# Order of the last mixture's gathers, its mix and three weight loads in the start of the last attention of a four-layer kernel

## What is computed

```python
x = x + tanh(g_xattn[i]) * xattn_i(layernorm(x), ctx)     # i = 0..3
x = x + tanh(g_ffn[i])   * ffn_i(layernorm(x))
```

## Time and profile before

| | before |
|---|---|
| median of 3 runs | 776.3 us (774.14 to 778.49) |
| the profiled execution, whole | 768.22 us |
| its span, first to last instruction | 766.1 us |
| mean granted TensorE clock | 0.925 of full |
| busy: PE / PE weight loads / DVE / ACT / POOL | 660.2 / 552.0 / 450.2 / 399.3 / 311.9 us |
| chain that ended last, by engine | PE 65%, DVE 18%, POOL 6%, issue 4%, ACT 3%, DMA 3% |
| the stretch in question | about 630 to 675 us of the 766 |

### The profile page before, as it was taken

How to read it: one execution, slowest core, us unless ns; L and a number is a source line. 1 busy time by engine, 2 the same in 40 slices (tenths; PEclk the granted TensorE clock), 3 DMA queues, 4 the chain that set the end, 5 groups by cost and what they waited for, 6 DMA issues and landing times.

```text
span 766.1 us, 17361 instructions
## 1 busy us (share of the span) xinstructions
PE 660.2 (86%) x6445; PEld 552.0 (72%) x6445; DVE 450.2 (59%) x1400; ACT 399.3 (52%) x977; POOL 311.9 (41%) x266
## 2 busy tenths in 40 slices
PE   3698997879989899899999999784699868999894
PEld 2487775779989777688887854563489857777684
DVE  5375768732223668575656677655433335779693
ACT  4565542355546565465656567321155745666471
POOL 4654430826234276132232347402234447654041
PEclk9699998699999999999999999985599988999997
DMA  6643680856776210000000020003357653521001
GB/s 169 162 99 90 195 241 2 245 154 173 219 223 188 85 31 25 1 2 1 1 1 2 1 83 1 1 0 96 116 138 228 174 161 98 144 56 37 3 15 42
DMA packets 60716, 70.92 MB, mean 93 GB/s; under 512 B 7051, under 2 KB 40859, under 8 KB 60635
## 3 DMA queue, kind: packets, MB, share of 16 engines
q1 hardware_dynamic: 57563, 63.52, 29.4%
q0 software_dynamic: 3072, 6.30, 2.7%
HBM read 48.89 MB, written 20.91 MB: 91 GB/s over the span
## 4 chain that ended last, share of the span: by engine, by line
PE 65%; DVE 18%; POOL 6%; issue 4%; ACT 3%; DMA 3%; SPq 0%; POOLq 0%; ACTq 0%; DVEq 0%
PE banks L1475 9%; PE banks L1491 8%; PE banks L1609 4%; PE banks L1312 3%; PE banks L1201 3%; PE banks L1618 3%; PE banks L1629 3%; PE banks L1289 3%; PE banks L1159 3%; PE banks L1161 2%; PE banks L1160 2%; PE banks L1267 2%; PE banks L1301 2%; PE banks L1661 2%; DVE rr L1955 2%
## 5 line engine op out<-in xcount | busy, mean ns | idle before, releaser
L994 ACT ACTIVATE hT<-banks,wup 128x128 f32<-128x128 f32 x304 | 86.8, 369 | 72.1 <-PE banks L1475 71.9
L913 ACT ACTIVATE pT<-banks 77x512 f32<-77x512 f32 x128 | 69.1, 591 | 54.8 <-PE banks L1289 54.4
L719 POOL DMA_INDIRECT xs<-xn,slot x48 | 47.0, 979 | 100.0 <-DVE ysb L2273 50.1
L624 POOL TENSOR_TENSOR kbd<-k,const 96x1248 fp32r<-96x1248 f32 x32 | 72.8, 2285 | 32.7 <-PE banks L1289 30.2
L1475 PE MATMUL banks<-xTs,wup 128*128 128x128 f32 x608 | 83.7, 283 | 2.1 <-issue 2.1
L1491 PE MATMUL banks<-wd,hT 128*128 x608 | 81.8, 279 | 0.6 <-ACT hT L994 0.3
L1475 PEld LDWEIGHTS banks<-xTs,wup 128*128 128x128 f32 x608 | 77.3, 200 | 3.0 <-issue 2.7
L679 POOL TENSOR_TENSOR sh<-sh,rd 128x616 f32<-128x616 f32 x32 | 39.0, 1218 | 98.8 <-DVE rd L1912 98.7
L2273 DVE COPY ysb<-banks 128x128 f32<-128x128 f32 x76 | 22.1, 291 | 91.7 <-PE banks L1491 91.7
L1491 PEld LDWEIGHTS banks<-wd,hT 128*128 128x128 f32 x608 | 74.7, 194 | 1.3 <-issue 1.1
L604 POOL TENSOR_TENSOR rstd<-vv,const 128x4 f32<-128x4 f32 x24 | 25.5, 1061 | 112.1 <-DVE vv L1859 111.8
(11 more groups left out here) (326 smaller groups left out, 1559.8 us busy)
## 6 DMA issues: line engine op xcount, KB each, us to landing
wup<-in_up SPq DMA_DIRECT2D x76, 258.0 KB, 3.3
q<-queries SPq DMA_DIRECT2D x21, 256.0 KB, 4.2
queries<-qc SPq DMA_DIRECT2D x8, 512.0 KB
wd<-in_down SPq DMA_DIRECT2D x8, 512.0 KB, 6.0
ys<-ysb SPq DMA_DIRECT2D x16, 256.0 KB
k<-keys SPq DMA_DIRECT2D x24, 156.0 KB, 3.6
xs<-zt SPq DMA_DIRECT2D x2, 1472.0 KB, 13.3
keys<-kc SPq DMA_DIRECT2D x8, 312.0 KB, 3.4
```

Source lines behind the costliest of these rows:

```text
L624: pool.tensor_tensor(kbd[b % NB8][0:96, :, :, :].bitcast(F32R), kb, m, ALU.mult).then_inc(h8.kbd, 1)
L719: pool.indirect_dma_start(xs[hh], bass.IndirectOffsetOnAxis(ap=idx[hh % 2][k_][:, t:t + 1], axis=0), xn8[hh % 2][:, t, :], None).then_inc( ...
L913: act.activation(pT[b % 2][0:SK, u, :], ps[0:SK, 2 + u % 2, :], ACT.Exp, scale=D8 ** -0.5)\
L994: ins = act.activation(hT[T % 3][:, c, :], ps[:, T % 2, c * P:c * P + P], func, bias=wup[T % NW][:, HID + c:HID + c + 1])
```

## The change

- POOL, run 1 only: at b = 0 it issues gathers 0 and 1, then `keys(1, 3)`, then gathers 2 and 3; at b = 1 there are no keys; at b = 2, after `keys(1, 4)`, it issues gathers 4 to 7, ahead of `rsqrt_front`.
- DVE: at b = 2 the mix of tiles 8 to 11 alone and a wait for its four instructions; at b = 4 the mix of tiles 12 to 15 and the wait for all of the mixture.
- SP: the three ternary loads with their waits move from group 1 (behind `query_roles(1, 1)`) to group 2 (behind `store_queries(1, 2)`, ahead of `query_roles(1, 2)`), and `query_roles` of every group now comes after that place.

```diff
                 store_queries(1, g)
-                query_roles(1, g)
-                if g == 1:
+                if g == 2:
                     wait_done(sp, "ff", 2)
                     sp.wait_ge(h8.st, 4 * (B + GB))
                     sp.dma_start(wfr[:, :], a["fc"]).then_inc(ld.l3, 16)
                     sp.dma_start(wpr[:, :, :], a["proj"]).then_inc(ld.l3, 16)
                     sp.dma_start(lnw[:, :, :], a["ln"]).then_inc(ld.l3, 16)
+                query_roles(1, g)
...
-                    if b + 2 < B and (b or run == 0):
+                    if b + 2 < B and (b >= 2 or run == 0):
                         keys(run, b + 2)
...
                         bias_rows(0, NG * phase, rows)
                         if run:
-                            collect(3)
+                            collect(3, 0, 4)
+                            keys(1, 3)
+                            collect(3, 1, 4)
+                    if run and b == 2:
+                        collect(3, 1, 2)
...
                     if b == 2 and between:
-                        between()
+                        between((0,), (0,))
+                        lk.wait()
+                    if b == 4 and between:
+                        between((0,), (1,))
                         wait_done(dve, "ff", 2)
...
-                def last_rows(choices=range(chosen(2 * run + 1)), parts=range(2)):
+                def last_rows(choices, parts=range(2)):
```

## The result

The changed kernel took 782.5 us (median of 8 runs, 780.8 to 785.9) beside 775.2 us (8 runs, 772.0 to 778.5) of the kernel before on the same chip: ratio 1.0094 [1.0072, 1.0117], **slower by 7.3 us**. The forecast was 778.8, its range ended at 782.0. The profiled execution took 783.6 us.

The account below looks back on a forecast made before the run. PE was taken as the bound, busy 86% of the span with 65% of the chain. Terms -0.59, -0.95, +0.8 and +3.2 summed to +2.5 us, put on the median of 776.3: 778.8 us, range 774.0 to 782.0.

Parts of the forecast that it names:

- `kbd` of b=3 earlier: PE at b=2: its wait for `kbd` of b=3, made by POOL after eight gathers, goes; 0.59 us gained.
- half the mix off the path at b=2: DVE at b=2: four mix instructions instead of eight bring `oT` earlier; 0.95 us gained on PE beyond the `kbd` gain.
- given back at b=3: At b=3: four gathers ahead of `rsqrt_front` leave it only 0.3 us earlier, so 0.8 us of PE's lead is lost.
- second mix held at b=4: DVE at b=4: two POOL instructions hold the four mix instructions, 3.9 us instead of 1.13; PE loses 3.2 us.
- Rival 1: At b=4: no hold, the four mix instructions take 1.13 us; -0.25 us in all, 776.0; chance 0.20.
- rival 2: At b=4: one hold only, DVE keeps going with all four mix instructions; +1.15 us, 777.5; chance 0.18.
- it decides when PE stands still much more than 3 us: Condition in rival 3: the clock's fall after PE's stand at b=5 decides only for stands much over 3 us.
- rival 3: PE's stand at b=5 makes the granted clock fall from 1.00 to 0.50; +6 us, 782.3; chance 0.06.
- of the same size: Evidence against rival 3: between 700 and 710 us PE was busy 7.22 of 10, with like waits, and kept 1.00.
- the gathers' neighbours: POOL's gathers at b=2: slowing of the mix beside them taken as zero, gather 3's data as hidden by 1 us.
- SP: SP's queue: earlier key transfers and later ternary loads and queries taken as zero, 0 to 1 us kept for the range.
- rival 4: Paired gathers or SP's later queries come late; the b=2 gain goes, 1 to 2 us added; about 780.5; chance 0.05.

Follow-up runs that it names:

- e1: The changed kernel once more, nothing altered, for a second profile: ratio 1.0037 against the kernel before on the same chip.
- e18: The changed kernel with all eight gathers at b=0 and the second mix piece ahead of b=4's second statistics step, repeating e14: ratio 0.9990 against the kernel before.
- e17: The changed kernel with four gathers at b=0 and then `keys(1, 3)`, four at b=2, second mix piece early as in e5: ratio 0.9979 against the kernel before.
- e5: The changed kernel with its second mix piece moved ahead of the second statistics step of b=4: ratio 0.9995 against the kernel before.
- e3: The changed kernel with the ternary loads left in group 1, so only gathers and mix changed: ratio 1.0067 against the kernel before.
- e10: The changed kernel with group 2's key transfers held until b=3's shifted scores, as before the change: ratio 1.0086 against the kernel before.
- e8: The changed kernel once more, nothing altered: ratio 1.0059 against the kernel before on the same chip.
- e12: The changed kernel with its second mix piece early, as in e5, on another chip: ratio 1.0064 against the kernel before.
- e13: The kernel before, unchanged, run against itself with a profile: ratio 0.9990.
- e16: The changed kernel once more, nothing altered, on the same chip as e13: ratio 1.0070 against the kernel before.
- e14: The changed kernel with all eight gathers at b=0 and the second mix piece ahead of b=4's second statistics step: ratio 0.9976 against the kernel before.
- e15: The changed kernel with all eight gathers back at b=0, the mix in two pieces where the change has it: ratio 1.0037 against the kernel before.
- e4: The kernel before with only the ternary loads moved to group 2, gathers and mix as before: ratio 0.9993 against the kernel before.
- e2: The kernel before, unchanged, run against itself for a second profile: ratio 1.0015.

## Why the prediction was wrong, step by step

On the chips where the kernel before takes 768 us each term of the sum can be set beside a difference of two stretches; they add up to the 1.77 us of e1 against before (85.11 - 83.34):

| term | forecast | measured |
|---|---|---|
| `kbd` of b=3 earlier | -0.59 | -0.61 (e18 to e17) |
| half the mix off the path at b=2 | -0.95 | -1.09 (before to e18) |
| given back at b=3 | +0.8 | +0.67 (e17 to e5) |
| second mix held at b=4 | +3.2 | +2.80 (e5 to e1) |
| sum | +2.5 | +1.77 |

**Right: the two gains.** Both to 0.14 us. The four instructions at b=2 took 1.13 us in every profile.

**Right in size, wrong in place: given back.** The forecast laid it to the four gathers ahead of `rsqrt_front`. e17 has those four and gives nothing back. It is the pair behind `keys(1, 3)`. In e1 POOL idles 3.51 us for PE ahead of `keys(1, 3)` and issues the pair only then; in e17 the pair goes out in that idle time, of which 1.15 us are left. In e1 it pushes the bias, `keys(1, 4)` and the four to the right, so that `rsqrt_front` starts at 651.63; in e17, without that pair in the way, POOL waits 0.46 us for DVE there. PE's wait of 0.48 us for ACT in e1 is the trace of it. The sum had the whole row of gathers in it, so its size came out.

**Right: the hold.** 3.44 to 3.45 us instead of the 3.9 of the forecast. Rival 1 (1.13) and rival 2 (2.5) fall: the bias got in between DVE's first and second instruction, as the sum had it. PE's stand isn't ended by the maxima that the forecast named but by `oT` (2.23 us), and only the 0.22 us behind it by the maxima. The step is 0.4 too big because the bias starts with the end of `kbd` (662.33 in e1) and not behind the first mix instruction, and what is left after it takes 0.67 us (663.65 to 664.32) and not 0.9.

**Wrong: "it decides when PE stands still much more than 3 us".** This is the step of rival 3 that failed, and its chance of 0.06 with it. No row stood behind that bound. The clock fell with stands of 2.23 and 0.22 us, two matmuls between them, in seven of nine profiles: from 0.4 us before the end of the long stand (e3) to 2.1 us behind it (e10). The evidence against it, waits "of the same size" between 700 and 710 us, was no such evidence. Timeline of PE of before:

```profile
703.22 0.49 PE L1321 MATMUL banks<-a_raw,oT 128*128 128x128 f32 x2 [1.04 <-DVE oT L1958]
704.53 0.56 PE L1267 MATMUL banks<-kbd,q 96*128 96x312 f32 x2 [0.81 <-DVE nm L1949]
...
710.51 0.49 PE L1321 MATMUL banks<-a_raw,oT 128*128 128x128 f32 x2 [1.43 <-DVE oT L1958]
```

These are three waits of 0.81 to 1.43 us, the stand at b=5 is one of 2.23, and it was forecast at 3. The price, 3.5 us for the clock, was near to the 2.8 measured. With it in the sum the profile gives +1.8 + 2.8 = +4.6 us, 0.6%. The changed kernel reads 1.0059, 4.5 us, on chip B (e8) and 1.0037, 2.8 us, on chip A (e1); the one profile of each kept the clock, so how many executions behind these medians lost it isn't shown.

**Wrong: the gathers' neighbours "costed at nothing".** The forecast asked whether a gather slows the mix (it doesn't) and whether its data come in time (they do), and not whether anything else slows beside it. On chip Y that is worth 3.9 us of the profile, on X n0 to n2 take 17.3 us (e12) where they took 10.7 on B (e5). No row of before bore it: by its time of 768.22 us, its profile came from a chip of the kind on which it doesn't happen. The median of before, 8 us above its own profile, was put on as a constant; it was the one sign of another kind of chip, and on such a chip the sum has another term.

On chip Y, from e13 to e16, the stretch grew by 8.35 us: -1.13 mix in two (e13 to e14), +5.58 hold and clock (e14 to e15), +3.90 gathers (e15 to e16). The medians beside them: -2.2 (against all 33 runs of before there; -0.6 against the 12 of e13), +5.6, +2.8. The first measurement's 7.3 us is of this kind.

**Right: SP.** The loads' new place costs and brings nothing as long as the mix is whole (e4). From 645 to 745 us neither PE nor DVE waits for a DMA in any profile of a kernel with the loads in the new place. Where they are in the old one, PE waits 0.25 us for `q` in e2, and 1.74 us at 675.56 in e3, the one kernel that has them there with the mix in two: there the new place saves a wait.

**A slip in the chances.** "All but rival 3 lie within 0.5% (3.9 us) of 776.3" leaves out rival 4: its 780.5 is 4.2 us off. No number of the forecast hangs on it.

**A version at least as good as both.** Gathers all at b=0, the mix in two pieces with the second one early (e14, e18) reads 0.9976 [0.9954, 0.9998] and 0.9990 [0.9970, 1.0011]; with four gathers late (e17) 0.9979 [0.9959, 0.9999]. That agrees with the 1.1 and 1.7 us of the stretches, 0.15 to 0.2%, which is at the edge of what these runs can tell. e17 wasn't run on a chip of the other kind.

## What to carry to other kernels

Before a VectorE step with two inputs in SBUF is moved, lay POOL's timeline over its new place: two tensor instructions there cost 2.3 us on four instructions of 0.28 us, and a few instructions earlier the same four cost nothing (e14, e18). Price a stand of PE with the clock in it, not only by its own length: here 2.2 us of standing cost up to 3.0 us more by the clock. And where a profile is faster than the median it is set against, ask what that chip hides, rather than add the difference as a constant.

## What the runs showed of the hardware that wasn't expected

On some chips (X, Y, and the first) DVE and ACT go on 3.1 to 4.3 us after the recorded end of the matmuls that they wait for, when POOL issues gathers beside PE's work; on others (A, B, C), with the same program and the same order, no such delay appears. It appears with the DMA engines at a share of 0.18 (e10) and not at 1.04 without gathers (e14). The kernel before has one such wait too, ahead of n0 (4.37 us in e13). PE's next instructions come late as well (2.30 us "issue" in after), so it may be PE's records that run ahead rather than its signals that lag; the profile can't tell these apart.

The clock fell around 2.45 us of standing in seven executions and not in two (e1, e8) that have the same waits: the same stand doesn't decide it alone.
